# Four layers on one core: the first layer's experts with their middle channels on partitions and its linear-attention products spread over the tiles; the third layer's gate by quarters

## The reference

```python
# layer 0: s is linear attention with a local convolution; f is this block
h = _layernorm(x + attn_out, ln1_g, ln1_b)          # gain and bias by channel
logits = flat @ router_w.T + router_b
_, top_i = jax.lax.top_k(jax.nn.softmax(logits, -1), 2)
assign = jnp.max(top_i, axis=-1)                     # one expert of 8 for a token
for e in range(E):
    he = jax.nn.gelu(flat @ w1[e].T + b1[e], approximate=False)   # 128 -> 128
    oe = he @ w2[e].T + b2[e]                                     # 128 -> 128
    out = jnp.where((assign == e)[:, None], oe, out)
return _layernorm(h + moe_out, ln2_g, ln2_b)

# layer 2: s is softmax attention in 8 batches of 256 tokens; f is this block
def step(c, xt):                                     # xt: 256 tokens, 8 steps
    ft = jax.nn.sigmoid(xt @ wf.T + c @ uf.T + bf)
    it = jax.nn.sigmoid(xt @ wi.T + c @ ui.T + bi)
    gt = jnp.tanh(xt @ wc.T + c @ uc.T + bc)
    return ft * c + it * gt, None
h = jnp.tanh(x @ wo.T + c_final @ uo.T + bo)         # then x = x + s * silu(h)
```

## Time and profile before

| what | value |
|---|---|
| median of 3 runs | 951.96 us (946.67 to 959.66) |
| profiled execution | 949.39 us, its span 947.9 us |
| busy of the span | PE 693.2 us, DVE 609.4 us, ACT 371.2 us, POOL 300.0 us |
| stretch of the experts of layer 0 | first transpose at 161.8 us, last scatter at 214.8 us |
| recurrence and lanes of layer 2 | 441.8 us to 517.9 us, then the gate to 527.6 us |

### The profile page before, as it was taken

One profiled execution on the slowest core, in us unless ns is written; L12 is line 12 of the kernel. 1 busy time (PEld: TensorE's weight loads), 2 busy tenths in 40 slices (PEclk: granted clock), 3 DMA queues, 4 the chain that ended last, 5 costly groups with the idle time before them and its releaser, 6 DMA issues.

```text
span 947.9 us, 14482 instructions
## 1 busy us (share of the span) xinstructions
PE 693.2 (73%) x4302; PEld 519.5 (55%) x4302; DVE 609.4 (64%) x1701; ACT 371.2 (39%) x918; POOL 300.0 (32%) x304
## 2 busy tenths in 40 slices
PE   4889867872588749424777497899997469989980
PEld 3889744752466638324666365566564434545650
DVE  5565767555779812187444763689993568984954
ACT  3101223142464323121434333477776235446662
POOL 2253325170000065300100200145552057775651
PEclk9999969595799969857999569899998579999996
DMA  9992001021100051218100734022220033225224
GB/s 295 225 253 113 2 12 49 21 75 45 44 1 1 1 45 19 73 31 351 65 1 1 165 80 110 7 75 70 82 69 2 0 67 80 78 60 161 74 59 136
DMA packets 79562, 73.49 MB, mean 78 GB/s; under 512 B 9617, under 2 KB 73884, under 8 KB 78848
## 3 DMA queue, kind: packets, MB, share of 16 engines
q1 hardware_dynamic: 55568, 52.48, 20.2%
q0 software_dynamic: 7072, 12.38, 5.3%
q10 hardware_dynamic: 16848, 7.73, 3.6%
HBM read 43.42 MB, written 27.42 MB: 75 GB/s over the span
## 4 chain that ended last, share of the span: by engine, by line
PE 29%; DVE 17%; DMA 4%; issue 3%; ACT 2%; SPq 1%; DVEq 1%; ACTq 0%; POOL 0%; POOLq 0%
PE banks L1015 4%; PE banks L2912 3%; PE banks L2482 2%; DVE work L3174 2%; PE banks L1008 2%; PE banks L2895 2%; PE banks L2346 1%; DVE work L2491 1%; PE banks L545 1%; PE banks L998 1%; PE banks L621 1%; PE banks L2734 1%; DVE work L3192 1%; DVE work L3176 1%; DMA work<-k_parts 1%
## 5 line engine op out<-in xcount | busy, mean ns | idle before, releaser
L1089 POOL DMA_INDIRECT ys<-work,back_to x101 | 102.9, 1018 | 76.0 <-ACT back_to L1034 37.7
L1015 PE MATMUL banks<-weights,work 128*128 x202 | 94.3, 551 | 0.2 <-ACT work L1031 0.2
L2491 DVE TENSOR_REDUCE work<-banks 128x2 f32<-128x512 f32 x128 | 83.0, 682 | 10.9 <-PE banks L2482 10.2
L1008 PE MATMUL banks<-weights,work 128*128 x358 | 63.0, 294 | 4.1 <-DVE work L1130 2.1
L998 PEld LDWEIGHTS banks<-consts,work 128*128 128x128 f32 x179 | 21.9, 144 | 68.2 <-DVE work L3192 38.1
L2482 PE MATMUL banks<-work 96*128 96x256 bf16 x256 | 49.2, 277 | 7.5 <-DVE work L2491 4.8
L771 POOL DMA_INDIRECT xs<-t,idx x48 | 50.0, 1042 | 14.8 <-issue 12.5
L1258 POOL DMA_INDIRECT g<-rows,back_to x16 | 15.3, 958 | 123.2 <-DVE back_to L1947 118.6
L1008 PEld LDWEIGHTS banks<-weights,work 128*128 128x128 f32 x358 | 48.6, 193 | 10.1 <-issue 7.4
L2895 PE MATMUL banks<-work 99*128 99x256 bf16 x256 | 48.4, 275 | 2.4 <-issue 2.3
L998 PE MATMUL banks<-consts,work 128*128 128x128 f32 x179 | 40.5, 297 | 13.2 <-DVE work L3192 5.3
(11 more groups left out here) (488 smaller groups left out, 1917.1 us busy)
## 6 DMA issues: line engine op xcount, KB each, us to landing
weights<-in_w SPq DMA_DIRECT2D x1, 6668.0 KB, 18.8
work<-xs ACTq DMA_DIRECT2D x101, 64.5 KB
xs<-zero SPq DMA_DIRECT2D x2, 2580.0 KB, 32.4
weights<-in_w SPq DMA_DIRECT2D x1, 4569.5 KB, 34.6
weights<-in_r SPq DMA_DIRECT2D x1, 2950.5 KB, 25.5
weights<-in_w SPq DMA_DIRECT2D x1, 2119.5 KB, 12.1
ys<-zero SPq DMA_DIRECT2D x1, 2048.0 KB, 28.9
g<-ys SPq DMA_DIRECT2D x8, 256.0 KB, 3.9
```

What stands on the lines that cost most here:

```text
L1008: ins = pe.matmul(bank(yb[m % len(yb)], 128), self.at_[m % 4][:, f * 128:(f + 1) * 128], self.w2[:, bass.ds(off[m] * NF + 128 * f, 128)], ...
L1015: pe.matmul(bank(mb + n % 4, F), self.hT[n % 4], self.w1[:, bass.ds(off[n] * (F // 128), F)], start=True, stop=True).then_inc(*self.prod1. ...
L1089: g.indirect_dma_start(self.ys[:, :], bass.IndirectOffsetOnAxis(ap=self.n.back_to[:, k:k + 1], axis=0), self.answer(n), None, bounds_check ...
L2491: v.tensor_reduce(self.mxb[:, 2 * h:2 * h + 2], self.n.bank(bank).rearrange("p (r n) -> p r n", r=2), AX, ALU.max, negate=True).then_inc(* ...
```

## The change

In layer 0:

- The norm before the router leaves out gain and bias. They are applied where the rows are turned (all four quarters of `Turn` then on ACT, by scale and bias of the activation), where an expert's tile is turned, and to the rows themselves in a new stage `GainRows`, eight DVE instructions woven with the experts.
- `GeluExperts` gets its own generators. The first product has the expert's weights as the stationary side and the turned tile as the moving one, so the middle channels come out on partitions: b1 becomes the bias of the Gelu, which reads PSUM, and its result is the stationary side of the second product without a transpose. DVE copies an expert's w1 out of its place for that. ACT reads the expert's number into a register for b1. Loads are issued by SP. The answer has 16 buffers.
- `LinearRows` yields after each pair of products on PE, and its DVE pieces stand five rounds apart.

In layer 2:

- The input products of a step move to a stage `RecurrenceInputs` at the end of the round before, and the states on DVE stand ahead of the lanes' piece.
- The output products have channels on partitions, 512 tokens each (one product and two), Tanh with the bias straight from PSUM, Silu by a second Tanh of half the value, and four transposes back for each quarter.
- `Gate` is gone: each quarter is multiplied by s and added to x on DVE when its transposes and its rows of s are there. `HeadFill` waits for the last quarter.

```diff
@@ class GeluExperts: pe
+        for n in range(N + 2):
+            if n < N:
+                off[n] = self.offset(pe, n)
+            m = n - 2
+            if m >= 0:
+                pe.wait_ge(*self.a.at(m))
+                if m >= len(yb):
+                    pe.wait_ge(*self.y.at(m - len(yb)))
+                pe.matmul(bank(yb[m % len(yb)], 128), self.aT[m % 4], self.w2[:, bass.ds(off[m], 128)], start=True,
+                          stop=True).then_inc(*self.prod2.up())
+            turn(n + 1)
+            if n < N:
+                pe.wait_ge(*self.xT.at(n))
+                pe.wait_ge(*self.copied.at(n))
...
+                pe.matmul(self.mid(n), self.wb[n % 4], self.hT[n % 4], start=True, stop=True).then_inc(*self.prod1.up())
+            yield
@@ act
+        for n in range(N):
+            turned(n + 1)
+            e = self.number(a, n)
...
+            a.activation(self.aT[n % 4], self.mid(n), ACT.Gelu, bias=self.b1[:, bass.ds(e, 1)]).then_inc(*self.a.up())
+            yield
@@ dve
+        copy(0)
+        copy(1)
+        for n in range(N + 3):
+            copy(n + 2)
+            m = n - 3
+            if m >= 0:
...
+                v.wait_ge(*self.prod2.at(m))
+                v.tensor_tensor(self.answer(m), self.n.bank(self.y_banks[m % len(self.y_banks)], 128), self.b2[:, bass.ds(off[m], 128)],
+                                ALU.add).then_inc(*self.y.up())
+            yield
@@ class LinearRows: pe
-            ins.then_inc(*self.out_mm.up())
+                if t == 3:
+                    ins.then_inc(*self.out_mm.up())
+                yield
             yield
@@ class LinearRows: dve
+        for _ in range(4):
+            yield
...
-            yield
+            for _ in range(5):
+                yield
@@ class GainRows: dve
+        for q in range(4):
+            t4 = n.t1[:, 4 * q:4 * q + 4, :]
+            v.tensor_tensor(t4, t4, grow(n.r0["ln1_g"], 4), ALU.mult).then_inc(*D.up())
+            k = D.now()
+            yield
+            v.wait_ge(*k)
+            v.tensor_tensor(t4, t4, grow(n.r0["ln1_b"], 4), ALU.add).then_inc(*D.up())
+            yield
@@ class Recurrence: pe
+        self.inputs(0)
         for t in range(8):
             for w, u, b in self.kinds:
+                pe.wait_ge(*(self.state.at(t - 1) if t else self.half.at(0)))
+                pe.matmul(n.bank(b, NS), w2[u], self.cc[t % 2], start=False, stop=True).then_inc(*self.gate_mm.up())
+            yield
@@ class Recurrence: dve, after the steps
+        for k in range(8):
+            if k < 4:
+                v.wait_ge(*self.z.at(k))
+                v.scalar_tensor_tensor(out=self.yT[k], in0=self.zb[k % 2], scalar=1.0, in1=self.yT[k], op0=ALU.add,
+                                       op1=ALU.mult).then_inc(*self.gT.up())
+            for q in ((0,), (1,), (2,), (), (), (3,))[k - 2] if k >= 2 else ():
+                for lane in self.lanes:
+                    v.wait_ge(*lane.rows.at(q))
+                v.wait_ge(*self.back.at(q))
+                g, x = n.g[:, 4 * q:4 * q + 4, :], n.x[:, 4 * q:4 * q + 4, :]
+                v.tensor_tensor(g, n.bank(4 + q).rearrange("p (r c) -> p r c", c=C), n.s[:, 4 * q:4 * q + 4, :], ALU.mult).then_inc(*D.up())
+                v.wait_ge(*D.now())
+                v.scalar_tensor_tensor(out=x, in0=g, scalar=0.5, in1=x, op0=ALU.mult, op1=ALU.add).then_inc(*self.made.up())
+            yield
@@ layer2
-    n.run(recurrence, *lanes)
+    n.run(recurrence, *lanes, RecurrenceInputs(n, recurrence))
-    gate = Gate(n, [recurrence.g.at(0), lanes[0].done(), lanes[1].done()])
-    fill.after = [recurrence.g.at(0), lanes[0].done(), lanes[1].done()]
+    fill.after = [recurrence.done(NT - 1)]
```

More of the change, by code:

```diff
@@ L608 @@
 class Router(Stage):
+    numbered = False
     def setup(self):
@@ new lines, in returned, with done, mid, sp @@
+    def returned(self, g):
+        every = len(self.row_out)
+        return self.row_out[g % every].at(4 * (g // every) + (3 if 4 * g + 4 <= self.TILES else 2))
+    def done(self):
+        groups = -(-self.TILES // 4)
+        return [self.returned(g) for g in range(groups - len(self.row_out), groups)]
+    def mid(self, n):
+        return self.n.bank(self.mid_bank + n % 4, 128)
+    def sp(self):
+        sp = self.sync
+        for s in self.sources:
+            sp.wait_ge(*s)
+        for n in range(self.TILES):
+            if n >= 4:
+                sp.wait_ge(*self.turned.at(n - 4))
+                sp.wait_ge(*self.to.at(n - 4))
+            sp.dma_start(self.rows[n % 4], self.xs[n * P:(n + 1) * P, :]).then_inc(*self.row_in[n % 4].up())
+        yield
@@ L1739, in layer0 @@
     n.run(sent, features)
[L1740 removed]
+    experts = GeluExperts(n, n.xs[0], n.ys[0], [sent.done(), route.tiles.at(1), features.kv.at(3)], n.w0["w1"], n.w0["w2"], n.w0["b1"],
+                          n.r0["b2"], n.w0["ln1_g"], n.w0["ln1_b"], 0)
     experts.turn_banks, experts.y_banks, experts.mid_bank = (2,), (7,), 3
     rows = LinearRows(n, features, conv)
[L1743 removed]
+    gained = GainRows(n, sent)
+    n.run(experts, rows, gained)
     got = Back(n, [n.g], n.ys[0], experts.done() + [rows.done()], "first")
@@ L2360, in act, with inputs, done @@
+    def inputs(self, t):
+        n, pe = self.n, self.tensor
+        for w, u, b in self.kinds:
+            pe.wait_ge(*(self.gates.at(3 * t - 3 + b - 4) if t else n.turn.done(0)))
+            pe.matmul(n.bank(b, NS), n.w2[w], n.xT[:, t, 1:1 + NS], start=True, stop=False)
+    def done(self, t):
+        return self.made.at(t // 4)
     def act(self):
@@ L2368, in act @@
             yield
-        for _ in range(9):
+        for j in range(4):
+            a.wait_ge(*self.out_mm.at(j))
+            a.activation(self.yT[j], n.bank(4 + j), ACT.Tanh, bias=n.w2["bo"]).then_inc(*self.y.up())
+            if j >= 2:
+                a.wait_ge(*self.gT.at(j - 2))
+            a.wait_ge(*self.y.at(j))
+            a.activation(self.zb[j % 2], self.yT[j], ACT.Tanh, scale=0.5).then_inc(*self.z.up())
             yield
-        a.wait_ge(*self.added.at(NT - 1))
-        a.activation(n.g[:, :, :], n.g[:, :, :], ACT.Tanh).then_inc(*self.g.up())
-        yield
     def dve(self):
```

216 lines of the change are left out of this document (122 added, 94 removed).

## The result

The changed kernel takes **920.3 us** (median of four runs, 917.9 to 928.9), the kernel before 952.4 beside it: ratio 0.968, 95% interval 0.958 to 0.977, faster by 3.2%. The profiled execution is the slowest of the four: 928.9 us, span 927.6 (granted clock 0.851; the other three have 0.858 to 0.864). Against the 947.9 of before that is 20.3 us, and this is what the two traces can explain; the other 12 us of the medians lie between executions.

What follows compares the result with a forecast made beforehand. It saw engines waiting in turn before the logits, PE then POOL pacing layer 0's experts, and a serial chain in layer 2. 949.4 - 5.0 - 3.9 - 12.9 - 7.5 = 920.1, forecast as 921, range 905 to 937.

Steps and rivals of the forecast that it cites:

- Layer 0 ahead of the router: Layer 0 before the experts: earlier turning and faster logits together gain 5.0 us (2.6 to 5.6).
- 2.4 us gained: Layer 0's logits: with PE's gap before the turning gone, a higher clock saves 2.4 us (bounds 0 and 3.0).
- Layer 0's experts: Layer 0's experts: less work per tile and paced pairs, with a wait on the answer's single bank, gain 3.9 us.
- two short ones of 0.6: End of layer 0's experts: after three rounds at 1.47, two short rounds of 0.6 us lead to the last scatter.
- The first rival: Layer 0's experts: the clock rises, rounds take 1.3 us, gain 14 us instead of 3.9, total 910; chance 0.25.
- The eight steps: Layer 2's recurrence: input products out of the chain and DVE's state ahead of the lanes gain 12.9 us.
- The second rival: Layer 2's steps: rounds do not get shorter, so the 12.9 us go, total 933; chance 0.20.
- The tail: Layer 2, last state to layer 3's statistics: 28.2 us instead of 35.8, gain 7.5 us (bounds 4 and 10).
- The fill: Fill on SP, now starting with layer 3's statistics: just hidden before the first store, costing 0 us, at most 2.
- The slow rival: Layer 2: the low clock holds, making it 31 us longer instead of 20.4 shorter, total 971; chance 0.04.

Runs made afterwards that it cites:

- e3: Changed kernel with two PSUM banks for the experts' answers (three instead of four for the middle): 965.5 us, ratio 0.968 to the kernel before.
- e5: The same kernel as e3, with two answer banks, run again in the next group: 966.3 us, ratio 0.958 to the kernel before.
- e2: Kernel before with only the layer-2 half of the change: 985.8 us, ratio 0.989 to the kernel before.
- e11: Changed kernel with two answer banks and DVE's four passes of a quarter's rows split over two rounds: 961.1 us, ratio 0.966 to the kernel before.
- e4: Changed kernel with the linear attention's pairs not paced, four in one round again: 975.2 us, ratio 0.980 to the kernel before.
- e10: Changed kernel with four unused products added behind every fourth linear-attention pair, where PE waits for DVE: 966.5 us, ratio 0.972 to the kernel before.
- e6: Changed kernel with layer 2's input products back in the same round, ahead of their state products: ratio 0.959 to the kernel before.
- e7: Changed kernel with DVE's state in layer 2 back behind the lanes' instructions: ratio 0.972 to the kernel before.
- e9: Changed kernel with both orders of layer 2's steps undone (input products in line, DVE's state behind the lanes), new tail kept: ratio 0.979 to the kernel before.
- e12: The changed kernel itself, run in the last experiment group: 965.3 us, ratio 0.970 to the kernel before.
- e1: Kernel before with only the layer-0 half of the change: 984.8 us, ratio 0.986 to the kernel before.

## Why the prediction was right

The forecast was 921, the median is 920.3, and the profiled pair differs by 20.3 us where the sum said 29.3. In the forecast's own terms the pair gives 2.7 + 3.0 + 13.0 + 7.3 = 26.0 of the 29.3, and 5.7 us are lost in code that the change does not touch (-3.3 + 0.4 - 2.8). That the median is still within 1 us of the forecast is chance: the profiled execution is 8.6 us above the median, and the other three, with a higher mean clock and without a trace, make good what the sum had too much. What the traces bear out is the mechanism, above all of layer 2, with 20.3 of the 26.0 us.

**Layer 0 ahead of the router, -5.0: too large, it was 2.7.** From the norm's first statistics to the logits it is 20.5 us instead of 22.7, in this trace and in those of all eleven experiments with this layer 0; so 2.2 of the 2.6 us of the earlier start are there. The term that failed is "2.4 us gained" on the logits: they take 6.49 us, not 4.5. The granted clock is 1.00 until 118 now and falls just there (0.61 in 118 to 122), though the gap ahead of the turning, on which the argument rested, has gone; ACT's four copies leave another of 1.77 us ahead of the logits. Ten of the twelve traces with this layer 0 have the logits at 6.0 to 6.6 us; in `e3` and `e5` the same code ran them in 4.5 and 4.0. The old layer 0 shows both as well, 6.97 in before and 4.7 in `e2`. So it is the clock that an execution gets, and no gain of the change; the bounds (2.6 to 5.6) had it, and I chose the wrong end.

**Layer 0's experts, -3.9: right in kind, 3.0.** The wait on the single bank came as reckoned: after the first four pairs the second product starts 3.3 us behind the fourth pair (3.4), the next time 2.9 (2.75). A period is 10.2 us (10.5). What was mis-sized is the end: the last rounds, said to be "two short ones of 0.6", are 1.47 each, since one bank lets no second product start before the answer. `e3`, `e5` and `e11` take the wait away (0.7, 2.6 to 3.1 and 3.8 us on their own chips), and `e4`, without the pacing, has waits of 3.3 us and 12 us more. What the first product's new orientation and the transpose left out give was not tried by itself.

**The first rival (the clock rises in the experts, 910)** did not come in the profile: the granted clock is mixed there, 0.50 in the dense rounds and up to 0.93 at the waits. Its price stays open. In `e10` the clock is 1.00 for 20 us and the rounds do fall to the rival's 1.3 (1.2 and 1.3), but E changes by 0.2 us, since a stop of 1.9 us on DVE follows in each period. Such stops stand in no trace of the first chip. The period of 9.6 us less PE's wait there is 7.8, and the rival had 8.4, 7.8 and 7.7. So on the chip of `e10` the 14 us are not there, and on the first chip no trace tests them. The Trainium skill ("TensorE: Matmul & The Clock Gate", section "What's actually happening") says that activity releases the throttle. `e10` agrees in direction, as added products lengthened the time at the higher level; but the changed kernel's own rows have 0.50 beside a PE busy 4.00 of 4 us.

**The eight steps, -12.9: right, 13.0.** The state products were to follow each other by 5.2, 4.3, 4.5, 4.4 us and came as 5.2, 4.3, 4.2, 4.5. ACT's exponentials hold up the Tanh of the round of C, as I had it, and cost 0.7 us over PE's 3.5 instead of 1.0. `e6`, `e7` and `e9` show the DVE order as the larger cause: alone it gives 13.4 of the 15.2 us. The half-sentence that the input products alone shorten the chain by 0.87 a step holds, beside the new DVE order, only in the short rounds (`e6`: 1.8 us in eight steps). The second rival (the rounds don't get shorter) is what `e9` is, and it needs both orders undone: 50.4 us, as the 49.4 of before.

**The tail, -7.5: right, 7.3.** 28.5 us against 28.2. Where the clock falls over PE's last products it is longer: 30.1 in `e4`, `e5`, `e10` and `e12`, so the low clock costs 1.6 there, within my 3, and 29.3 to 29.9 in `e6`, `e7` and `e9`.

**The fill, 0: right.** The first store comes 15.4 us after the statistics and immediately behind the fill. It follows the fill's end by 0.04 us, so nothing of the cover is left: were the store's input ready sooner, it would have to wait for the fill.

**The slow rival** (low clock through layer 2) did not come: in all eleven traces with the new order, or with one half of it, the clock is high through all eight steps. Only `e9` and `e1`, with both orders old, have a dip of one step. What no step named is layer 3, code that the change does not touch: the two traces differ there by -2.8 us, with 3.6 us lost behind the first experts' last middle pass, where the second experts begin, and 0.8 won ahead of it. Its granted clock is 0.53 in the changed kernel (the first row) and 0.72 in the one before (the second), in one execution each:

```profile
830.00:836.00 6.00, 5.27 (x9) 2.31 (x10) 0.42 (x1) 2.38 (x10) 3.68 (x4) 0.53 0.26 70
```

```profile
854.00:860.00 6.00, 5.78 (x14) 2.76 (x15) 1.13 (x3) 3.44 (x14) 4.47 (x5) 0.72 0.30 78
```

## To carry to other kernels

Two orders in one loop can overlap, when one engine's late result holds the other's instructions in a fixed queue. Undone one by one they cost 1.8 and 7.5 us here, made one by one they gave 7.7 and 13.4, and together 15.2. So measure a pair in both directions, and undo both, before saying what either gave. Where a result has a single PSUM bank, whatever stands ahead of its reader on the other engine is in the chain: 2.1 us of passes in one piece stood behind waits of 2.1 to 2.7 us in each period, and a second bank with the passes in two rounds gave 3.8 us. A higher granted clock makes the rounds shorter, but only the period counts: in `e10` rounds fell from 1.9 to 1.3 us and an unexplained stop took it all back. Look for the next wait before counting on the clock.

## What was not expected of the hardware

**Layer 3's first experts on other chips.** The same code (39 tiles, first to last middle pass on DVE) takes 77.9 and 78.9 us in the two shown traces and 110.4 to 112.3 in all twelve of the experiments, on three chips. The 33 us lie in the first part, while POOL sends its scatters without pause: PE, DVE and ACT have long stops. The changed kernel as `e12`, then in its own profile:

```profile
776.00:782.00 6.00, 2.77 (x9) 1.89 (x9) 1.68 (x5) 1.15 (x4) 4.78 (x5) 0.50 0.23 68
782.00:788.00 6.00, 0.69 (x1) 0.00 (x0) 0.23 (x1) 0.00 (x0) 4.48 (x6) 0.50 0.17 56
```

```profile
776.00:782.00 6.00, 5.46 (x27) 2.91 (x26) 5.13 (x16) 3.12 (x12) 4.75 (x5) 1.00 0.34 86
782.00:788.00 6.00, 5.63 (x29) 3.04 (x28) 5.36 (x15) 3.12 (x12) 4.51 (x5) 1.00 0.31 77
```

The stops of 1.7 to 3.9 us in layer 0's experts, where POOL's scatters follow each other at 1.28 us, are seen on the same three chips and not on the first, where the kernel before sent 19 scatters in a row at about 1.3 us without one. That both have one cause is only argued, and what it is stays open.

**The granted clock in two stages.** In layer 0's experts it is 0.50 in two stretches with PE busy 4.00 of 4 us and 0.93 in the one between them with PE busy 1.88 of 4; in layer 2 it is 1.00 from 440 to 500 with PE busy 56.5 of 60 us. What tells the two apart was not found.
